# The last residual add of a two-layer attention and expert kernel, split between the vector engine and GpSimd

## What is computed

```python
router_logits = xf @ gate_w
topk_vals, topk_idx = jax.lax.top_k(router_logits, TOP_K)      # TOP_K = 2 of 8 experts
topk_w = jax.nn.softmax(topk_vals, axis=-1)
comb = comb.at[jnp.arange(n_tokens)[:, None], topk_idx].add(topk_w)
h = jax.nn.gelu(jnp.einsum('nd,edf->enf', xf, W1) + b1[:, None, :], approximate=False)
y = jnp.einsum('enf,efd->end', h, W2) + b2[:, None, :]
out = jnp.einsum('ne,end->nd', comb, y)
...
x = x + _L1_ffn_ref(_layernorm(x, axis=-1), L1_ffn_gate_w, L1_ffn_W1, L1_ffn_b1, L1_ffn_W2, L1_ffn_b2)
```

## Time and profile before

| what | us |
|---|---|
| three runs | 460.85, 457.23, 460.57 |
| their median | 460.57 |
| the profiled execution | 459.19 |
| its span, first to last instruction | 457.0 |

### The profile page before, as it was taken

The page is one execution under the profiler, slowest core; times in us unless marked ns, Lnnn a source line. Parts: engine busy times, 40 slices in busy tenths (PEclk is TensorE's granted clock), DMA queues, the critical chain, the costliest instruction groups (busy, mean ns, idle before and its releaser), DMA issues.

```text
span 457.0 us, 12684 instructions
## 1 busy us (share of the span) xinstructions
PE 367.4 (80%) x4442; PEld 261.4 (57%) x4442; DVE 347.6 (76%) x989; ACT 270.1 (59%) x601; POOL 267.6 (59%) x342
## 2 busy tenths in 40 slices
PE   4777988897679999999987999888642599999900
PEld 3544666665336656565654577666522388888900
DVE  6785699998867786889777489888655399999806
ACT  3573788885255555565567688666421277667604
POOL 8950377776655559595850255387777136676640
PEclk9897699998589999999999599888655599999975
DMA  7277991000001111110014100000011222322127
GB/s 207 61 217 205 363 380 39 3 3 2 1 1 47 48 48 46 47 47 1 1 21 62 17 1 4 1 32 25 31 43 55 83 60 85 95 79 78 48 74 236
DMA packets 30836, 33.13 MB, mean 73 GB/s; under 512 B 3908, under 2 KB 22606, under 8 KB 30776
## 3 DMA queue, kind: packets, MB, share of 16 engines
q1 hardware_dynamic: 27692, 26.11, 19.9%
q0 software_dynamic: 2496, 5.18, 3.3%
q10 hardware_dynamic: 588, 1.05, 0.6%
HBM read 15.22 MB, written 15.01 MB: 66 GB/s over the span
## 4 chain that ended last, share of the span: by engine, by line
PE 52%; DVE 15%; POOL 14%; issue 9%; ACT 5%; DMA 3%; SPq 1%; POOLq 0%; DVEq 0%; ACTq 0%
PE ps L1249 10%; PE ps L1251 9%; PE ps L1250 9%; PE ps L1418 6%; POOL sorted_rows L712 5%; PE ps L1339 4%; DVE area L934 3%; PE ps L1370 2%; PE ps L1313 2%; POOL expert_sums L758 2%; POOL area L738 1%; PE ps L1548 1%; ACT vals L417 1%; POOL area L695 1%; POOL area L657 1%
## 5 line engine op out<-in xcount | busy, mean ns | idle before, releaser
L738 POOL TENSOR_TENSOR area<-area 128x512 f16<-128x512 f32 x44 | 50.9, 1157 | 34.1 <-ACT area L538 33.9
L758 POOL DMA_INDIRECT expert_sums<-area x46 | 47.4, 1030 | 37.8 <-ACT area L557 27.8
L1249 PE MATMUL ps<-w,area 128*128 128x128 f16 (+1 forms) x360 | 63.8, 219 | 0.9 <-POOL area L738 0.8
L1249 PE MATMUL ps<-area,w 128*128 128x512 f16 (+1 forms) x180 | 60.5, 336 | 4.7 <-DVE area L1135 3.1
L1251 PE MATMUL ps<-w,area 128*128 128x128 f16 (+1 forms) x360 | 63.8, 219 | 0.0
L1250 PE MATMUL ps<-w,area 128*128 128x128 f16 (+1 forms) x360 | 63.8, 219 | 0.0
L1251 PE MATMUL ps<-area,w 128*128 128x512 f16 (+1 forms) x180 | 60.2, 335 | 0.0
L1250 PE MATMUL ps<-area,w 128*128 128x512 f16 (+1 forms) x180 | 60.2, 334 | 0.0
L934 DVE TENSOR_REDUCE area<-ps 128x8 f32<-128x512 f32 x64 | 41.3, 687 | 18.0 <-PE ps L1418 17.1
L534 ACT ACTIVATE area<-ps 128x512 f32<-128x512 f32 x44 | 26.2, 597 | 38.5 <-PE ps L1548 37.9
L1131 DVE SCALAR_TENSOR_TENSOR area<-ps,area 128x512 f32<-128x512 f32 x44 | 30.1, 685 | 17.6 <-ACT area L534 17.6
(11 more groups left out here) (222 smaller groups left out, 1050.0 us busy)
## 6 DMA issues: line engine op xcount, KB each, us to landing
sorted_rows<-filler_rows SPq DMA_DIRECT2D x16, 528.0 KB, 6.2
w_stage<-in_L_ffn_W SPq DMA_DIRECT2D x8, 512.0 KB, 4.0
w<-sorted_rows SPq DMA_DIRECT2D x23, 132.0 KB
keys<-area SPq DMA_DIRECT2D x32, 48.0 KB
area<-in_ctx SPq DMA_DIRECT2D x4, 256.0 KB, 3.8
x_res<-in_x SPq DMA_DIRECT2D x4, 256.0 KB, 4.8
keys<-expert_sums SPq DMA_DIRECT2D x4, 256.0 KB, 5.4
keys<-expert_sums ACTq DMA_DIRECT2D x4, 256.0 KB, 5.9
```

Source lines behind the costliest of these rows:

```text
L738: nc.gpsimd.tensor_tensor(hid[:, n % 4, 1, :], gated[:, n % 4, :], hid[:, n % 4, 0, :], ALU.subtract).then_inc(q["lo"], 1)
L758: nc.gpsimd.indirect_dma_start(out=expert_sums, out_offset=bass.IndirectOffsetOnAxis(ap=to_row[:, j, h:h + 1], axis=0), in_=ys[j % OUTS][: ...
L1249: pe.matmul(dst, lhs[0], rhs[0], start=start, stop=False, **kw)
```

## The change

Of the two adds of scaled rows in each group, the one for the group's first two tiles stays on DVE, and the one for its third and fourth tile goes to GpSimd, behind GpSimd's last scatter. A new semaphore, `padd`, counts GpSimd's adds. DVE makes x + p0*s0 for the third and fourth tile of a group first and for the first and second tile after them. SP issues the outputs in the same order as before, but waits for `padd` at every second one.

```diff
@@ SP
-                    sp.wait_ge(q["add"], (G + 2) * g + G + h + 1)
+                    if h == 0:
+                        sp.wait_ge(q["add"], (G + 1) * (g + 1))
+                    else:
+                        sp.wait_ge(q["padd"], g + 1)
                     sp.dma_start(out_dram[:, t0:t0 + 2, :], x[:, t0:t0 + 2, :]).then_inc(s["out_d"], 16)
@@ GpSimd, after the last scatter
+            for g in range(GROUPS):
+                t0 = G * g + 2
+                pool.wait_ge(q["add"], (G + 1) * g + 2)
+                pool.wait_ge(q["wq"], t0 + 2)
+                nc.gpsimd.tensor_tensor(x[:, t0:t0 + 2, :], x[:, t0:t0 + 2, :], sums[:, 1, t0:t0 + 2, :], ALU.add).then_inc(q["padd"], 1)
@@ DVE
                 for g in range(GROUPS):
                     dve.wait_ge(SUM[g], 32)
-                    for t in range(G * g, G * g + G):
+                    for n in (2, 3, 0, 1):
+                        t = G * g + n
                         nc.vector.scalar_tensor_tensor(x[:, t, :], sums[:, 0, t, :], prob[:, t, 0:1], x[:, t, :], ALU.mult, ALU.add).then_inc(q["add"], 1)
-                    for h in range(2):
-                        t0 = G * g + 2 * h
-                        dve.wait_ge(q["add"], (G + 2) * g + G + h)
-                        dve.wait_ge(q["wq"], t0 + 2)
-                        nc.vector.tensor_tensor(x[:, t0:t0 + 2, :], x[:, t0:t0 + 2, :], sums[:, 1, t0:t0 + 2, :], ALU.add).then_inc(q["add"], 1)
+                    t0 = G * g
+                    dve.wait_ge(q["add"], (G + 1) * g + G)
+                    dve.wait_ge(q["wq"], t0 + 2)
+                    nc.vector.tensor_tensor(x[:, t0:t0 + 2, :], x[:, t0:t0 + 2, :], sums[:, 1, t0:t0 + 2, :], ALU.add).then_inc(q["add"], 1)
```

More of the change, by code:

```diff
@@ L248, in build @@
                   + ("xd xt_lo oh cb c16 ct_ps ct_a ct_d res t1 gt", "a16 rk_ps rk bs place tbl b1_ps b1 slots_ps xs_hi xs_lo gate y "
-                     "tok nm wq sc ld0 ld1 ld2 ld3 so0 so1 so2 so3 so4 so5 so6 so7 sum0 sum1 sum2 sum3 add")[l], f"_f{l}") for l in range(2)]
+                     "tok nm wq sc ld0 ld1 ld2 ld3 so0 so1 so2 so3 so4 so5 so6 so7 sum0 sum1 sum2 sum3 add padd")[l], f"_f{l}") for l in range(2)]
         LD = [F[1][f"ld{n}"] for n in range(LOADS)]
```

## The result

The change made the kernel slower, and its median lies above the whole range of the prediction: 465.25 us as the median of four runs (463.92 to 466.74), against 460.45 before (457.23 to 460.85). The ratio is 1.0131, with a 95% interval from 1.008 to 1.0182. I had forecast 460.0, a range up to 461.6, and no measurable change.

A forecast was written before the change was run, and what follows sets the result against it. DVE was taken to bound the last 8 us. Four stops of 0.48 us (1.92) less 1.37 for saved adds gave +0.55 us on a mean of 459.46, so 460.0 us, range 457.4 to 461.6.

The forecast's parts named there:

- What bounds the tail: Final combination: DVE bounds the last 8 us, with ACT's scalings and the loads ahead of it.
- What the change removes: DVE's second add of groups 0 to 2: 3 x 0.46 = 1.37 us off, if nothing holds DVE up.
- the arrival of group 2: Loads of group 2 in the tail: waiting for its rows takes at most 0.06 us of the gain.
- The GpSimd add: Each of four new 256-column fp32 adds in the tail takes 0.67 us, bounds 0.58 and 1.58.
- The stop of DVE: In the tail, each GpSimd add holds up DVE's two-input SBUF instructions for 0.48 us, bounds 0 and 1.39.
- The rival without a stop: In the tail, GpSimd's and DVE's instructions run side by side, stop 0, time 458.1 us; chance 0.2.
- The rival in which GpSimd waits for gaps: In the tail, GpSimd gets the port only where DVE leaves a gap; three stops count, +0.07, 459.5 us; chance 0.2.
- The sum: Last output of the tail is issued 4s - 1.37 later; with stop s of 0.48, 1.92 - 1.37 = +0.55 us.
- Landing and the rest stay as they are: After the last output's issue, nothing changes, so the +0.55 us passes unchanged to the kernel's time.
- GpSimd's own chain ends nothing: GpSimd's four adds, 2.7 us, lie beside 6 us of DVE and end the kernel by less than one add.
- slow rival: In the tail, each GpSimd add takes 1.58 us and stops DVE for 1.39: +4.2, 463.7 us; chance 0.06.

The follow-up runs named there:

- the two kernels without it: Changed kernel with GpSimd's four adds taken out (tail 9.16 us, single run 461.07 us); changed kernel with each add replaced by a GpSimd memset (tail 12.75 us).

## Why the prediction was wrong

- **What bounds the tail** (DVE, with ACT and the loads ahead of it): right for the outputs. It was incomplete, since the span ends when the last engine has drained, and I followed only SP's outputs.
- **What the change removes** (0.46 us for each of the groups 0 to 2): right. Without the stop, groups are 1.51 us apart, and the outputs of the two kernels without it are issued at 6.56 and 6.81 instead of 7.98 (1.42 and 1.17 off, where 1.37 was forecast). The smaller one is due to the arrival of group 2. The larger one has 0.04 more because SP's second output of a group followed the first by 0.42 there, and by 0.46 before.
- **The GpSimd add** at 0.67 us: 0.72 undisturbed, 0.73 to 0.77 beside DVE. The straight line between 16 and 512 columns was 0.05 low (its slope is 936 / 496 = 1.887, not 1.885, which changes nothing). Whether that comes from the fp32 result, from the kind of instruction or from a cost that isn't linear in the columns, no run tells.
- **The stop of DVE** at 0.48 us for each add: measured 807 - 347 = 0.46 to 816 - 347 = 0.47, four times in 16 products. The first two adds both hit group 1, in its first and its fourth product. The rival without a stop falls. That the size came out is partly luck. The prediction took the stop as GpSimd's duration less 0.19; with the 0.76 that the adds took this is 0.57, and the last output would have been 4 x 0.57 - 1.37 = 0.9 later instead of 0.47. In the trace the stretched product began some 0.10 behind GpSimd's add (451.67 and 451.78 for the first) and was held until 0.20 before that add's end: 0.76 - 0.10 - 0.20 = 0.46. The 0.19 itself was a misreading: at 197.82 DVE had come 0.04 after GpSimd, and its stop ended at 197.82 + 0.97 = 198.79, which is 0.15 before GpSimd's end, as in the other instance. The rival in which GpSimd waits for gaps falls too: its records are 0.73 to 0.77 and the stretched products stand in the middle of the stream.
- **The sum** of +0.55 us for the last output: 8.45 instead of 7.98 into the tail, +0.47.
- **The step that failed** is the sentence "Landing and the rest stay as they are", together with "GpSimd's own chain ends nothing. It ends the kernel only if DVE is done first, and then by less than one add". I took GpSimd's last add for the end of its chain. Behind it stands its closing drain, 6.47 us, which before was over 0.58 us into the final combination. Moving GpSimd's last instruction from 5.9 us ahead of DVE's first product to 7.4 us behind it put the drain at the end, with 464.36 for the span instead of the 460.67 + 0.4 = 461.1 that SP's end would have given (460.67 is SP's branch in the closing line, which stood 0.4 ahead of the span's end before): 3.3 us. The prediction's slow rival reached 463.7, by another mechanism (adds of 1.58 us) that isn't there; it doesn't count for it.
- 0.5 us from the stop and 3.3 from the drain are the 3.8 us by which the tail grew. The rest of the 4.8 between the two first medians is not explained by any run, and lies within their uncertainty.

## What to carry to other kernels

Before giving an engine that has finished early a little more work at the end, look at what stands behind its last instruction, in the rows of the program's closing line: a drain that begins early and ends under other work is a price that moves with the engine's last instruction. On GpSimd this drain grew with the number of indirect transfers that the program had issued, 0.082 us for each, so after many of them the last GpSimd instruction should end that much ahead of the kernel's end. And a GpSimd add that reads SBUF stopped DVE, which was running instructions with two SBUF inputs, for 0.46 of its 0.76 us, so that moving an add of 0.46 us there brought nothing even where the drain was hidden.

## What I had not expected of the hardware

GpSimd's closing drain ended 0.07, 3.85, 6.45 to 6.47 and 7.60 us after its last instruction in programs with 0, 46, 78 and 92 indirect transfers from it. Its length did not depend on what the last instruction was (add, memset, or the last scatter itself), nor on how long ago the transfers had been made, since it had its full 6.45 and 6.47 us even where the last instruction came 14 and 13 us after the last of them. In the profile it shows only in the rows of the closing line and as an idle wait of SP that names another engine.
